# Local attention in a hybrid kernel: softmax division moved behind the value product

## The reference

```python
q, k, v = (proj_chunk(W, b) ...)              # Bx, S=16, H=16, SEG=64, DK=8
out = _attn(q, k, v)                          # softmax over the segment's own 64 keys
kd, vd = k[:, :, :, ::4, :], v[:, :, :, ::4, :]   # 16 keys of a segment
for off in (1, 2):
    for sign in (-1, 1):
        n = seg_ids + sign * off
        cross = _attn(q, kd[:, n], vd[:, n])  # a softmax of its own over 16 keys
        out = out + jnp.where(valid, cross * 0.25, 0.0)
return out @ Wo + bo
```

## Time and profile before

| what | value |
|---|---|
| median of 3 runs | 1217.64 us (1215.99 to 1227.82) |
| the profiled execution | 1218.06 us |
| its span, first to last instruction | 1216.2 us |
| mean granted TensorE clock | 0.979 of full speed |
| TensorE, VectorE, ScalarE, GpSimd busy | 91%, 76%, 67%, 19% of the span |
| local attention, first scores to last output | 779.5 to 1037.3 us |

### The profile page before, as it was taken

How to read it: one execution, slowest core, us unless ns; L and a number is a source line. 1 busy time by engine, 2 the same in 40 slices (tenths; PEclk the granted TensorE clock), 3 DMA queues, 4 the chain that set the end, 5 groups by cost and what they waited for, 6 DMA issues and landing times.

```text
span 1216.2 us, 20248 instructions
## 1 busy us (share of the span) xinstructions
PE 1112.6 (91%) x7444; PEld 619.4 (51%) x7452; DVE 925.7 (76%) x1513; ACT 816.4 (67%) x1300; POOL 234.8 (19%) x332
## 2 busy tenths in 40 slices
PE   7898899999999989989999899898888888898987
PEld 3343344444444445467765344466666666463354
DVE  4868788777777677857775577699999896576965
ACT  5868665555555664755576645888888776868774
POOL 1000000000000001200000012487878776000000
PEclk9999999999999999989999999899999998999999
DMA  6000112222211000000000000000000000000002
GB/s 175 1 0 1 48 61 65 61 65 63 63 62 61 26 1 0 10 1 2 2 1 1 1 1 8 1 3 2 2 3 2 15 2 2 9 1 1 0 1 70
DMA packets 26363, 27.19 MB, mean 22 GB/s; under 512 B 4172, under 2 KB 17309, under 8 KB 26269
## 3 DMA queue, kind: packets, MB, share of 16 engines
q1 hardware_dynamic: 25936, 25.91, 7.2%
q10 hardware_dynamic: 332, 0.01, 0.0%
HBM read 23.30 MB, written 2.62 MB: 21 GB/s over the span
## 4 chain that ended last, share of the span: by engine, by line
PE 62%; DVE 16%; ACT 13%; issue 6%; POOL 1%; DMA 0%; SPq 0%; ACTq 0%; DVEq 0%
PE psum L741 8%; PE psum L730 8%; PE psum L733 4%; PE psum L990 4%; PE psum L87 4%; PE psum L962 3%; PE psum L1641 2%; PE psum L1972 2%; DVE arena L2158 2%; PE psum L1389 2%; DVE N L2167 2%; ACT ln_std L114 2%; ACT ln_std L116 2%; PE psum L105 2%; DVE arena L1449 1%
## 5 line engine op out<-in xcount | busy, mean ns | idle before, releaser
L769 ACT ACTIVATE arena<-psum 128x512 f32<-128x512 f32 x128 | 69.5, 594 | 112.9 <-PE psum L730 112.9
L730 PE MATMUL psum<-arena,weights 128*128 128x512 f32 x256 | 120.8, 594 | 1.7 <-DVE N L128 1.0
L741 PE MATMUL psum<-arena,weights 128*128 128x512 f32 x256 | 120.3, 592 | 0.0
L627 DVE SCALAR_TENSOR_TENSOR arena<-diff,vecs,N 128x512 f32<-128x512 f32 x128 | 95.1, 745 | 0.0
L689 DVE SCALAR_TENSOR_TENSOR arena<-arena,psum 128x512 f32<-128x512 f32 x64 | 44.0, 687 | 61.2 <-PE psum L741 61.2
L2072 ACT ACTIVATE N<-N 128x1024 f32<-128x1024 f32 x64 | 67.8, 1059 | 32.2 <-DVE N L2167 31.5
L1982 PE MATMUL psum<-ident,N 128*128 128x128 f32 x512 | 73.0, 288 | 13.0 <-POOL N L2127 12.4
L741 PEld LDWEIGHTS psum<-arena,weights 128*128 128x128 f32 x256 | 48.6, 190 | 61.2 <-issue 61.2
L730 PEld LDWEIGHTS psum<-arena,weights 128*128 128x128 f32 x256 | 48.0, 190 | 62.0 <-issue 57.6
L1972 PE MATMUL psum<-arena 32*128 32x128 f32 x1024 | 77.4, 291 | 1.6 <-ACT arena L2050 1.4
L2068 ACT ACTIVATE arena<-psum 128x1024 f32<-128x1024 f32 x64 | 65.6, 1024 | 19.0 <-PE psum L1982 18.8
(11 more groups left out here) (332 smaller groups left out, 2506.8 us busy)
## 6 DMA issues: line engine op xcount, KB each, us to landing
arena<-tw_rows SPq DMA_DIRECT2D x64, 256.0 KB, 3.1
out_dram<-arena SPq DMA_DIRECT2D x8, 256.0 KB, 3.6
...
```

Source lines behind the costliest of these rows:

```text
L627: op = nc.vector.scalar_tensor_tensor(mixed[:, n % 4, a, :], k.diff[:, q % 2, :], k.vec((f"cm_k{e}", f"cm_r{e}")[a]), before, ALU.mult, AL ...
L730: op = nc.tensor.matmul(k.bank[2 * (n % 2) + h][:], k.eWk[:, e, h * P:(h + 1) * P], mixed[:, n % 4, 0, :], start=True, stop=True)
L741: op = nc.tensor.matmul(k.bank[4 + n % 2][:], k.eWv[:, e, h, :], ks[:, (2 * (n % 2) + h) * CH:(2 * (n % 2) + h + 1) * CH], start=(h == 0), ...
L769: op = nc.scalar.activation(kr[:, h * CH:(h + 1) * CH], k.bank[2 * (n % 2) + h][:], ACT.Relu)
```

## The change

The exponential no longer works in place ahead of everything else. The shifted scores are turned first, and ScalarE's exponential reads the turned scores from PSUM and writes `pT`. Nothing is divided before the value product. Instead, the values of each segment are laid out by group: `apart` on GpSimd writes `vx`, for each of 16 heads 5 x 8 columns (the values times a mask of the group's keys, a quarter in it for the four neighbours) and 5 columns of ones under the same masks. The turned scores are now the weights of the value product (64 columns), the 45 columns of `vx` are moving, and for each head and query the result has five partial products of 8 and five sums. ScalarE takes Ln of the sums and copies the products out of PSUM, then Exp; GpSimd multiplies 320 columns by the reciprocals (`weigh`); VectorE adds the five groups (`sums`, 320 to 64 columns) into `ot`; for two units together TensorE transposes the result and ScalarE copies it to `ov` (`heads`). The score buffers `pr` are two instead of four, `pT` three instead of two. The values' read-out is one copy instead of four with a scale, the memsets of `ln_sq` and `ln_std` go, the masks `sg_own` and `sg_share` are made in `segment_loads`, and the output weights come in one transfer in their plain order. The transposes work on unit n-2; projections, turned values, outputs and the addition to `X` have new places. The diff without `segment_loads`, the start of the stage, and names of semaphores:

```diff
-    SEG, NSEG, T2 = 64, L // 64, 16
+    SEG, NSEG, GROUPS = 64, L // 64, 5
     N = B * NSEG
     TURNS = N // 8
     AROUND = (-2, -1, 1, 2)
-    pr = [k.N[:, i * 8 * P:(i + 1) * 8 * P] for i in range(4)]
-    pT = [k.arena[:, 16 * 1024 + i * 8 * P:16 * 1024 + (i + 1) * 8 * P] for i in range(2)]
+    pr = [k.N[:, i * 8 * P:(i + 1) * 8 * P] for i in range(2)]
+    pT = [k.N[:, 2 * 8 * P:3 * 8 * P]] + [k.arena[:, 16 * 1024 + i * 8 * P:16 * 1024 + (i + 1) * 8 * P] for i in range(2)]
     ov = [k.arena[:, 18 * 1024 + i * CH:18 * 1024 + (i + 1) * CH] for i in range(2)]
     mx = [k.arena[:, 19 * 1024 + i * 40:19 * 1024 + (i + 1) * 40] for i in range(2)]
-    sm = [k.arena[:, 19 * 1024 + (2 + i) * 40:19 * 1024 + (3 + i) * 40] for i in range(4)]
-    hs = [k.mixed[:, i, 0, 0:256].rearrange("p (h n) -> p h n", h=8) for i in range(2)]
-    vt = [v[:].rearrange("p s (h n) -> p s h n", h=4) for v in (k.ln_sq, k.ln_std)]
+    sm = [k.arena[:, 19 * 1024 + (2 + i) * 40:19 * 1024 + (3 + i) * 40].rearrange("p (h g) -> p h g", h=8) for i in range(4)]
+    ot = [k.arena[:, 19 * 1024 + 256 + i * P:19 * 1024 + 256 + (i + 1) * P] for i in range(2)]
+    kept = k.ln_std[:].rearrange("p w n -> p (w n)")
+    ev = [kept[:, i * 320:(i + 1) * 320].rearrange("p (h g d) -> p h g d", h=8, g=GROUPS) for i in range(3)]
+    wt = [kept[:, (3 + i) * 320:(4 + i) * 320] for i in range(2)]
+    vt = [k.ln_sq[:, i, :].rearrange("p (s h d) -> p s h d", s=4, h=16) for i in range(2)]
+    spare = k.mixed[:].rearrange("p a j n -> p (a j n)")
+    vx = [spare[:, i * 720:(i + 1) * 720].rearrange("p (h n) -> p h n", h=16) for i in range(4)]
     scored = [k.pair[0], k.pair[1]]
     turned_to, weighed_to, other = k.pair[2], k.bank[6], k.bank[7]
+    weighed_by_head = weighed_to[:, 0:360].rearrange("p (h n) -> p h n", h=8)
+    heads_to = weighed_to[:, 360:360 + P]
...
-    PROJ = {0: 0, 1: 1, 3: 2, 4: 3, 7: 4, 11: 5}
+    PROJ = {0: 0, 2: 1, 3: 2, 4: 3, 10: 4, 12: 5}
 
     def project_at(n):
-        return (n // 16 + 1) * 6 + PROJ[n % 16] if 2 <= n < N - 16 and n % 16 in PROJ else None
+        return (n // NSEG + 1) * 6 + PROJ[n % NSEG] if 3 <= n < N - NSEG and n % NSEG in PROJ else None
 
     def values_at(n):
-        return n // 4 if n < N and n % 4 == 2 else None
+        return n // 4 if n < N and n % 4 == 1 else None
 
     def output_at(n):
-        return (n - 13) // 8 if n >= 13 and n % 8 == 5 else None
+        return (n - 15) // 8 if n >= 15 and n % 8 == 7 else None
...
         def turned(n):
-            pe.wait_ge(k.sg_mul, n + 1)
+            pe.wait_ge(k.sg_arg, n + 1)
             if n >= 1:
-                pe.wait_ge(k.sg_pT, n)
+                pe.wait_ge(k.sg_exp, n)
             for e in range(8):
-                op = nc.tensor.transpose(turned_to[:, e * P:(e + 1) * P], pr[n % 4][:, e * P:(e + 1) * P], k.ident[:])
+                op = nc.tensor.transpose(turned_to[:, e * P:(e + 1) * P], pr[n % 2][:, e * P:(e + 1) * P], k.ident[:])
             op.then_inc(k.sg_turned, 1)
 
         def weighed(n):
-            u, half = n // 2, n % 2
-            pe.wait_ge(k.sg_pT, n + 1)
-            pe.wait_ge(k.sg_vt, n // 4 + 1)
-            if n % 8 == 0 and n >= 8:
-                pe.wait_ge(k.sg_ov, n // 8)
-            for s in range(2):
-                for r in range(2):
-                    for h in range(4):
-                        op = nc.tensor.matmul(weighed_to[32 * h:32 * (h + 1), (u % 4 * 2 + s) * SEG:(u % 4 * 2 + s + 1) * SEG],
-                                              vt[n // 4 % 2][:, u % 2 * 2 + s, h, (2 * half + r) * 24:(2 * half + r) * 24 + 32],
-                                              pT[n % 2][:, (r * 2 + s) * 256 + h * SEG:(r * 2 + s) * 256 + (h + 1) * SEG],
-                                              start=(n % 8 == 0 and s == 0 and r == 0), stop=(half == 1 and r == 1), skip_group_check=True)
+            pe.wait_ge(k.sg_exp, n + 1)
+            pe.wait_ge(k.sg_vx, n // 2 * 2 + 2)
+            if n == 0:
+                pe.wait_ge(k.sg_first, 4)
+            if n >= 1:
+                pe.wait_ge(k.sg_ev, n)
+            if n >= 5 and n % 2 == 1:
+                pe.wait_ge(k.sg_ov, (n - 3) // 2)
+            for r in range(2):
+                for j in range(2):
+                    for h in range(2):
+                        for s in range(2):
+                            e, slot = r * 4 + s * 2 + j, r * 4 + j * 2 + h
+                            op = nc.tensor.matmul(weighed_to[s * SEG:(s + 1) * SEG, slot * 45:(slot + 1) * 45], pT[n % 3][:, e * P + h * SEG:e * P + (h + 1) * SEG],
+                                                  vx[(n // 2 * 2 + s) % 4][:, n % 2 * 8 + slot, :], start=True, stop=True)
             op.then_inc(k.sg_pv, 1)
+
+        def heads(p):
+            pe.wait_ge(k.sg_sum, 2 * p + 2)
+            pe.wait_ge(k.sg_ev, min(2 * p + 4, N))
+            if p >= 1:
+                pe.wait_ge(k.sg_ov, p)
+            nc.tensor.transpose(heads_to, ot[p % 2], k.ident[:]).then_inc(k.sg_oT, 1)
...
         def output(t):
             free()
-            pe.wait_ge(k.sg_ov, t + 1)
+            pe.wait_ge(k.sg_ov, 4 * t + 4)
             nc.tensor.matmul(other[:], k.sg_wo, ov[t % 2], start=True, stop=True).then_inc(k.sg_out, 1)
             last.append((k.sg_x, t + 1))
 
         first()
-        for n in range(N + 6):
+        for n in range(N + 8):
             if n < N:
                 scores(n)
-            if 0 <= n - 3 < N:
-                turned(n - 3)
+            if 0 <= n - 2 < N:
+                turned(n - 2)
+            if n >= 8 and n % 2 == 0:
+                heads((n - 8) // 2)
             if 0 <= n - 4 < N:
...
         def values(v):
             act.wait_ge(k.sg_vT, v + 1)
-            if v == 0:
-                act.wait_ge(k.sg_quarters, 3)
             if v >= 2:
-                act.wait_ge(k.sg_pv, 4 * v - 4)
-            for s in range(4):
-                to = vt[v % 2][:, s].rearrange("p h (r n) -> p r h n", n=32)[:, :, :, 0:8]
-                op = nc.scalar.activation(to, other[:, s * P:(s + 1) * P].rearrange("p (r h d) -> p r h d", r=4, h=4), ACT.Identity, scale=k.sg_quarter)
-            op.then_inc(k.sg_vt, 1)
-
-        def turned(n):
+                act.wait_ge(k.sg_vx, 4 * v - 4)
+            nc.scalar.activation(vt[v % 2].rearrange("p s h d -> p (s h d)"), other, ACT.Copy).then_inc(k.sg_vt, 1)
+
+        def exp(n):
             act.wait_ge(k.sg_turned, n + 1)
-            if n >= 2:
-                act.wait_ge(k.sg_pv, n - 1)
-            nc.scalar.activation(pT[n % 2], turned_to, ACT.Copy).then_inc(k.sg_pT, 1)
-
-        def exp(n):
-            act.wait_ge(k.sg_arg, n + 1)
-            nc.scalar.activation(pr[n % 4], pr[n % 4], ACT.Exp).then_inc(k.sg_exp, 1)
+            if n >= 3:
+                act.wait_ge(k.sg_pv, n - 2)
+            nc.scalar.activation(pT[n % 3], turned_to, ACT.Exp).then_inc(k.sg_exp, 1)
 
         def weight(n):
-            act.wait_ge(k.sg_sum, n + 1)
-            nc.scalar.activation(sm[n % 4], sm[n % 4], ACT.Ln).then_inc(k.sg_ln, 1)
+            act.wait_ge(k.sg_pv, n + 1)
+            if n >= 3:
+                act.wait_ge(k.sg_mul, n - 2)
+            nc.scalar.activation(sm[n % 4], weighed_by_head[:, :, 40:45], ACT.Ln).then_inc(k.sg_ln, 1)
+            nc.scalar.activation(ev[n % 3].rearrange("p h g d -> p h (g d)"), weighed_by_head[:, :, 0:40], ACT.Copy).then_inc(k.sg_ev, 1)
             act.wait_ge(k.sg_ln, n + 1)
             nc.scalar.activation(sm[n % 4], sm[n % 4], ACT.Exp, scale=-1.0).then_inc(k.sg_weight, 1)
 
-        def heads(t):
-            act.wait_ge(k.sg_pv, 8 * t + 8)
-            if t >= 2:
-                act.wait_ge(k.sg_out, t - 1)
-            nc.scalar.activation(ov[t % 2], weighed_to, ACT.Copy).then_inc(k.sg_ov, 1)
+        def heads(p):
+            act.wait_ge(k.sg_oT, p + 1)
+            if p >= 8:
+                act.wait_ge(k.sg_out, p // 4 - 1)
+            nc.scalar.activation(ov[p // 4 % 2][:, p % 4 * P:(p % 4 + 1) * P], heads_to, ACT.Copy).then_inc(k.sg_ov, 1)
...
-        for n in range(N + 6):
-            if n >= 12 and n % 8 == 4:
-                heads((n - 12) // 8)
-            if 0 <= n - 3 < N:
-                turned(n - 3)
-            if n < N:
-                exp(n)
-            if 0 <= n - 1 < N:
-                weight(n - 1)
+        for n in range(N + 8):
+            if 0 <= n - 2 < N:
+                exp(n - 2)
+            if 0 <= n - 4 < N:
+                weight(n - 4)
+            if n >= 8 and n % 2 == 0:
+                heads((n - 8) // 2)
...
-        def halve(n):
-            mine, others = split(pr[n % 4])
-            pool.wait_ge(k.sg_exp, n + 1)
+        def apart(n):
+            pool.wait_ge(k.sg_vt, n // 4 + 1)
+            if n >= 4:
+                pool.wait_ge(k.sg_pv, n // 2 * 2 - 2)
+            nc.gpsimd.tensor_tensor(vx[n % 4][:, :, 0:40].rearrange("p h (g d) -> p h g d", g=GROUPS),
```

(65 more changed lines are left out.)

42 lines of the change are left out of this document (25 added, 17 removed).

## The result

The changed kernel takes 1229.06 us in the median of 20 runs (1220.19 to 1232.06) against 1220.76 for the kernel before in as many runs beside it. The ratio is 1.0053, with a 95% interval of 1.0033 to 1.0073. The forecast of 1224 us against 1217.64 was 1.0052. So a change that in 62 us of its stage takes 12 to 16 us of work off each of VectorE, ScalarE and GpSimd makes the kernel half a per cent slower.

A forecast was written before the change was run, and what follows sets the result against it. VectorE was taken to bound the stage before, TensorE after the change. The 59 steps add 7.4 us, the tail gives back 1.6: 1218.06 us becomes 1223.9, said as 1224 us, range 1200 to 1246.

The forecast's parts named there:

- Which engine waits: Local attention: VectorE's plain unit falls from 3.43 to 2.90 us, TensorE's rises from 2.70 to 3.20; they change places.
- The price of the product: TensorE's value product per unit: 32 records bound by loading, two tiles side by side, 1.09 us where it was 0.59.
- moving-bound rival: Value product: loads hide behind the other tile's work, block 0.77 us, kernel 1205 us; chance 0.13.
- serial one: Value product: loading and moving one after the other in a tile, block 1.66 us, kernel 1258 us; chance 0.10.
- the 0.14 us: TensorE's blocks: what a score block or value product costs beyond its records, 0.14 us.
- The waits: TensorE on the shared PSUM bank: 2.2 us before turned values three times, 1.1 us before a projection twice; 8.9 in all.
- a case of their own: TensorE's clock falls to half behind the 2.2 us waits, three falls, 10 to 12 us more, 1235 us; chance 0.08.
- The other terms: Per unit: GpSimd 2.3 us, up to 3.1, costed at nothing; ScalarE loses some 0.5 us and is no bound.
- heads' transpose: TensorE's new 128 x 128 transpose of finished heads for every two units: 0.17 us each, 28 make 4.8 us.
- 59 steps: Local attention from unit 4 to unit 63: 233.5 us by TensorE's work and waits against 226.1, +7.4.
- The tail: From the end of the last shift to the last output: 10.9 us instead of 12.5, giving back 1.6.
- The first units: Local attention's first four units keep their time: TensorE at half clock in half of them, first waits for the same projections.

The follow-up runs named there:

- Experiment 6: Changed kernel with VectorE's sum of 320 elements done a second time into a spare tile, 0.40 us more per unit; 1223.2 us, ratio 1.0015 to the kernel before.
- experiment 3: Changed kernel with each value product cut in two of 32 weight columns, so four column tiles; 1212.56 us, ratio 0.9952 to the kernel before.
- 8: Changed kernel with 32 instead of 64 weight columns in each value product from unit 2 on, leaving out half the queries; 1206.61 us, one run.
- 7: Changed kernel with 24 instead of 45 moving columns in each value product, leaving out part of the result; 1374.21 us, one run.
- 9: Changed kernel with queries' read-out earlier, addition to X ahead of the maxima, and 24 of 45 columns moved; 1210.84 us against 1216.91 before, one run each.
- 5: Changed kernel with queries' read-out earlier, addition to X ahead of the maxima, and four column tiles; 1198.62 us, ratio 0.9794 to the kernel before.
- 10: Changed kernel with queries' read-out earlier, addition to X ahead of the maxima, four column tiles, and 24 of 45 columns moved; 1192.48 us, one run.
- experiment 1: Changed kernel with ScalarE reading the second half of a query projection at the next unit's start, ahead of the exponential; 1219.45 us, ratio 0.9978 to the kernel before.
- 2: Changed kernel with queries' read-out earlier and VectorE's addition to X ahead of the same unit's maxima; 1217.57 us, ratio 0.9979 to the kernel before.

## Why the prediction was right, step by step

**Which engine waits.** Right. In the kernel before the units follow VectorE, afterwards TensorE. For the kernel before this rests on the rows alone; no run there changed the work of either engine in a unit. Experiment 6 shows it from the one side (0.40 us more on VectorE in each unit: nothing), experiments 3 and 8 from the other (0.27 and 0.29 less on TensorE: 12 and 13 us, short of 16 and 17 by the time at the lower clock level and by waits that grew).

**The price of the product.** Right, 1.07 us for 1.09, and for the reason given: bound by loading two tiles that work side by side. The moving-bound rival (0.77) and the serial one (1.66) fall with experiments 7 and 8. The products can be set side by side by what one tile gets, taking off the 0.14 us that the prediction found beyond the records:

| weight columns / moved, tiles | block us | records per tile | us a record in its tile |
|---|---|---|---|
| 64 / 45, two (after) | 1.07 | 16 | 0.058 |
| 64 / 24, two (7, 9) | 1.05 | 16 | 0.057 |
| 32 / 45, two (8) | 0.78 | 16 | 0.040 |
| 32 / 45, four (3, 5) | 0.80 | 16 | 0.041 |
| 32 / 24, four (10) | 0.68 | 16 | 0.034 |
| 32 / 64, four (before) | 0.59 | 8 | 0.056 |

Two tiles or four makes no difference to a tile (0.040 and 0.041): they don't disturb each other. In five of the six rows a record in a tile costs about the longer of its load and its move, not their sum: with 64 weight columns the load (0.057), with 32 the move of 45 (0.040, where 45/64 of the old 0.056 is 0.039). The sixth, 32 / 24, lies above that: its move would be 0.021 (24/64 of 0.056) and its load, as half of 0.057, 0.029, and it takes 0.034; why is open. All rows assume the same 0.14 us beyond the records. This is also why experiment 3 gains: it loads as many columns, but over four tiles instead of two.

The Trainium skill's rule for the load (TensorE: Matmul & The Clock Gate, section LDWEIGHTS) gives 53 ns for 64 columns, and the measured 0.057 us is near it; the prediction's estimate of a block by this rule, 0.99 us, would have been 0.08 short. The Trainium skill's other rule (the same page, section Part 3, The mechanism), that loads hide behind moves only where the row group differs, would make a record 0.057 + 0.039, since every product here uses all 128 rows; it takes 0.058, so the runs disagree.

**The waits.** Right in place, number and size: three of 2.09 us (2.2 said) and two of 1.18 (1.1 said). Experiments 1 and 2 take them away one kind after the other. What the sum left out is that a wait can also cost clock. I had given the falls a case of their own at 10 to 12 us; they came, behind two waits of five, but at 1.5 us each.

**The other terms.** The heads' transpose adds 0.11, not 0.17, 1.7 us less in all. GpSimd and ScalarE by groups, forms apart, against the earlier trace rows:

```profile
L2140 POOL TENSOR_TENSOR mixed<-ln_sq,weights 128x640 f32<-128x640 f32 x64 | 83.8, 1311 | 8.5 <-ACT ln_sq L2085 8.5
...
L2098 ACT ACTIVATE ln_std<-psum 128x320 f32<-128x320 f32 x64 | 27.6, 432 | 0.0
```

1311 ns for 640 elements where 1.21 us was said, 432 for ScalarE's copy where 0.45 was; with 35 of 62 us GpSimd was no bound, as assumed. So the sum of the 59 steps can be closed: 233.5 - 1.2 (product) - 1.7 (heads) - 0.3 (waits) + 3.1 (clock) = 233.4, and 233.6 was measured. That the forecast met it to 0.1 us is partly luck: two small misses of opposite sign.

**The tail** is the step that failed, by 2.8 us. I counted one transpose block and three products behind the last shift; the timeline has two and four, 2.0 us more. The rest of an output that still runs when the shift ends adds 0.3, and two transposes of heads between the products 0.4. The order of TensorE's loop gives this count: behind the scores of unit 63 it turns unit 61, weighs unit 59 and starts an output before it turns unit 62. That takes it until 1032.78, and VectorE's shift ends at 1032.45. TensorE was not nearer to the end before; three transpose blocks and four products stood behind the last shift there, with waits for other engines between them:

```profile
1024.17 1.88 PE L1982 MATMUL psum<-ident,N 128*128 128x128 f32 x8 [0.19 <-ACT arena L2068]
...
1027.85 1.09 PE L1982 MATMUL psum<-ident,N 128*128 128x128 f32 x8 [1.22 <-POOL N L2127]
...
1031.28 1.04 PE L1982 MATMUL psum<-ident,N 128*128 128x128 f32 x8
```

**The first units** took what was said, 15.3 us for 15.6 from the first scores to the maxima of unit 4, but not because the change leaves them alone. The same distance is 11.3 us in experiment 6, at a clock of 1.00 from 781 to 790 us, and 17.1 in experiment 1, where the low level lasted longest.

**The whole.** The forecast ratio of 1.0052 met the measured 1.0053 closer than its parts did. Of the 11.0 us between the two profiled executions, 5.8 had been forecast (7.4 less 1.6); the tail is 2.8 of the difference, and the 2.6 us ahead of the first scores and behind the last output (1.5 and 1.1) lie in stages that the change doesn't touch. That the ratio agrees to 0.0001 is luck.

**TensorE busy for over 95% of the stretch** was said; it is 94.7%, because this stretch has two of the five waits in it.
